# A two-layer graph attention kernel: weights loaded during the tables, the first layer's weights prepared on GpSimd, first gathers released by their indices alone

## The chip, the cores and the metric

One core of a Trainium2 chip runs the kernel. The metric is device time in microseconds from start to end of one execution. The core's engines run their own instruction streams and meet at semaphores: TensorE (PE, matrix products and transposes), VectorE (DVE), ScalarE (ACT), GpSimd (POOL) and SyncE (SP, which here only issues transfers). SP, ACT and GpSimd each issue DMA transfers, which run on the same 16 DMA engines.

## The reference

A graph has 12500 nodes with 256 features and 200000 edges, sorted by destination, each with one of 64 types. Two attention layers with 4 heads of 64 follow one another, each inside a residual sum and a layer norm.

```python
# layer 0, typed edges
enh = x + 0.1 * query_emb
Q, K, V = enh @ Wq + bq, enh @ Wk + bk, enh @ Wv + bv        # (N, 4, 64)
scores = einsum("ehd,ehd->eh", Q[dst], K[src] + 0.2 * rel_w[type]) / 8
w = segment_softmax(scores, dst)
msgs = segment_sum(w * V[src], dst)
x0 = layernorm(msgs @ Wo + bo + x) * gamma + beta
x = layernorm(x + x0)
# layer 1, plain edges and a loop on each node
xp = x @ W
alpha = leaky_relu((xp * att_src).sum(-1)[src] + (xp * att_dst).sum(-1)[dst], 0.2)
out = elu(segment_sum(segment_softmax(alpha, dst) * xp[src], dst) + bias)
x = layernorm(x + out)
```

## The kernel before

The kernel runs four stages one after another. Each is a `Stage`, which allocates its SBUF and PSUM tensors and semaphores; at its end all engines meet at a barrier and its semaphores are cleared. Tensors of the object `k` (`Kernel`) live through all four.

1. `make_tables` reads the edge lists as 105 rows of 1920 edges and makes the tables on which the later gathers work: `k.idx` (source indices by tile, turned by TensorE and copied by VectorE, L496), `k.first_row` and `k.match` (to HBM). A chain of checks ends in `k.flag` (L511). SP issues all loads (L429 to L435), ScalarE makes one cast (L460), GpSimd has no work.
2. `project_nodes` (98 blocks of 128 nodes) computes keys, values and queries. SP first issues eight weight loads (L547 to L553), then waits for VectorE's fill of `zero` (L631) and goes into its loop of x loads (L560), stores and clears of the sums. VectorE waits for all eight weights, spreads the query vector (L635); TensorE multiplies it by the weights (L608, L612) to fold it into the biases, and after VectorE's last scaling of the biases TensorE's loop begins with the transposes at L587. GpSimd adds beta to each x block (L672), into `k.x1`.
3. `attend_typed` is the first layer, over 521 tiles of 384 edges. GpSimd gathers three times 128 rows of `k.kv` per tile (L765) into one of eight row buffers; the ninth tile's gather waits until TensorE has aggregated the first. SP fetches index slices (L777), queries (L785), edge types and match rows (L801, L804). The order of each engine's work is written out by `interleave`: parts with a lag in tiles, and parts per node block every four or eight tiles that finish the block (norms, products with `Wo` and `W`).
4. `attend_plain` is the second layer, with the same gather scheme over `k.xp` (L1286).

What the change touches is how stage 3 starts. ScalarE issues its twelve weight loads as the stage opens (L1192 to L1201). VectorE fills buffers (L1080 to L1085), waits for all twelve, and prepares: the relation weights split in bfloat16 parts `rel_a`, `rel_b` (L1087 to L1100), the two biases in three bfloat16 rows each (L1103 to L1113, with fused multiply-adds), four products of `W` with the attention vectors (L1116) and two reductions of them into extra columns of `w1` (L1120). Each step waits for the one before it. Then VectorE raises `setup`, for which all the other engines wait ahead of their first step, GpSimd ahead of the first gather and SP ahead of the first query fetch:

```python
pool.wait_ge(setup, 1)
interleave(pool, FIRST, TilePart(0, gather))
```

## Time and profile before

| | us |
|---|---|
| median of three runs | 4633.29 |
| the three runs | 4626.58, 4633.29, 4635.58 |
| the profiled execution | 4628.61 |
| its span, first to last instruction | 4627.2 |

The stages as the timeline of that execution shows them:

| stage | opens at | first work of its main loop |
|---|---|---|
| tables | 1.02 | 8.30 (VectorE's chain) |
| projections | 30.03 | 44.75 (TensorE) |
| typed layer | 330.18 | 350.64 (first gather) |

A row of the timeline gives start, duration, engine, line of the kernel, operation, output and inputs with their sizes, how many instructions were merged (x4), and in brackets how long the engine had been idle and what released it. SPq, ACTq and the like are an engine's queue of DMA issues; their time is that of the issue, not of the transfer. A row of windows gives for each engine its busy time and instructions, in the order PE, PE's weight loads, VectorE, ScalarE, GpSimd, then the granted TensorE clock as a share of full speed, the DMA engines' busy share and the rate in GB/s. A row of a DMA queue gives packets, MB and the share of the 16 engines' time over the stretch. A row of waits gives who waited for whom, total time, times and longest.

### The profile page before, as it was taken

Reading aid. Unit: us, or ns where it says so; the run is one execution under the profiler, and the core shown is the slowest. Engines: PE = TensorE matmul, PEld = TensorE weight load, DVE = VectorE, ACT = ScalarE, POOL = GpSimd, SP = SyncE. Lnnn points to the kernel's source line nnn. Section 1 sums busy time; section 2 is a strip of 40 time slices with the busy share of each in tenths; the row PEclk is TensorE's granted clock in tenths of the full one; section 3 lists DMA queues with packets and bytes.
Section 4 is the critical chain, followed back from the end, with each engine's and each line's share of the span. In section 5 each row is a group of like instructions: output and inputs, shape, how many; then the busy total and the mean of one; then the engine's idle time right before and its main releaser. Section 6 shows DMA issues by size and latency. Waiting matters only on the chain. (4 is left out here: it accounts for less than half of the span.)

```text
span 4627.2 us, 149696 instructions
## 1 busy us (share of the span) xinstructions
PE 3929.3 (85%) x42462; PEld 2568.6 (56%) x42462; DVE 3415.2 (74%) x11602; ACT 2795.2 (60%) x7985; POOL 3143.2 (68%) x3229
## 2 busy tenths in 40 slices
PE   6988999999999999999996778778877877777874
PEld 4655555555555555555554556555555555555553
DVE  3235788777777778777775578888778778787777
ACT  2324555555555555555553677777777777777775
POOL 1217777777777777777772777777777777777773
PEclk9998999999999999999997677777778777787777
DMA  6878888888888888888884777777777777777774
GB/s 207 282 236 246 259 259 259 257 259 259 259 255 260 258 260 258 257 258 261 259 256 120 187 206 206 207 204 205 207 207 205 205 204 205 205 208 209 203 206 131
DMA packets 820558, 1052.06 MB, mean 227 GB/s; under 512 B 458633, under 2 KB 632338, under 8 KB 820464
## 3 DMA queue, kind: packets, MB, share of 16 engines
q0 software_dynamic: 225072, 726.83, 53.9%
q1 hardware_dynamic: 594078, 323.35, 27.0%
q10 hardware_dynamic: 1314, 0.99, 0.1%
q14 instruction: 80, 0.66, 0.0%
q8 instruction: 14, 0.23, 0.0%
HBM read 915.79 MB, written 133.39 MB: 227 GB/s over the span
## 5 line engine op out<-in xcount | busy, mean ns | idle before, releaser
L1286 POOL DMA_INDIRECT plain_rows<-xp,plain_index x1563 | 1559.8, 998 | 554.9 <-issue 440.8
L765 POOL DMA_INDIRECT typed_rows<-kv,typed_index x1563 | 1511.2, 967 | 626.2 <-issue 414.3
L1391 PE MATMUL plain_p_o<-plain_rows,plain_weight_t 128*64 128x130 f32 (+1 forms) x8336 | 856.5, 348 | 44.0 <-DVE plain_weight_t L1417 43.3
L1158 ACT ACTIVATE typed_weight<-typed_weight,typed_col 128x416 f32<-128x416 f32 x521 | 334.6, 642 | 855.0 <-DVE typed_col L991 809.5
L1378 PE MATMUL plain_p_s<-all_cst,plain_rows 128*128 128x128 f32 (+1 forms) x2084 | 455.0, 318 | 368.2 <-DMA plain_rows<-xp,plain_index 365.9
L1391 PEld LDWEIGHTS plain_p_o<-plain_rows,plain_weight_t 128*64 128x64 f32 (+1 forms) x8336 | 570.2, 169 | 203.8 <-issue 128.5
L1378 PEld LDWEIGHTS plain_p_s<-all_cst,plain_rows 128*128 128x128 f32 (+1 forms) x2084 | 335.2, 174 | 522.6 <-issue 504.8
L989 DVE CUSTOM_DVE_ANT_0 typed_weight<-typed_p_s,typed_far 128x416 f32<-128x416 f32 x521 | 305.1, 586 | 371.5 <-PE typed_p_s L874 347.8
L874 PE MATMUL typed_p_s<-typed_kt,typed_q 64*32 64x416 f32 x4168 | 472.4, 521 | 103.4 <-issue 73.0
L1424 DVE CUSTOM_DVE_ANT_0 plain_alpha<-plain_alpha,plain_far 128x416 f32<-128x416 f32 x521 | 310.0, 595 | 311.4 <-ACT plain_alpha L1540 296.4
L962 DVE TENSOR_TENSOR typed_kt<-typed_p_kt,typed_rel 128x768 f32<-128x768 f32 x521 | 494.7, 950 | 3.7 <-PE typed_p_kt L851 3.4
L1548 ACT ACTIVATE plain_weight<-plain_alpha,plain_col 128x416 f32<-128x416 f32 x521 | 331.4, 636 | 256.2 <-DVE plain_col L1433 250.4
L851 PE MATMUL typed_p_kt<-all_cst,typed_rows 128*128 128x128 f32 x3126 | 458.4, 283 | 6.8 <-DMA typed_rows<-kv,typed_index 6.3
L1559 ACT COPY plain_result<-plain_p_o 32x65 f32<-32x65 f32 x2084 | 425.4, 204 | 18.2
L889 PE MATMUL typed_p_o<-typed_rows,typed_weight_t 128*32 128x65 f32 (+1 forms) x16672 | 413.4, 225 | 3.0 <-ACT typed_result L1165 0.4
L1363 PE MATMUL plain_p_w<-all_cst,plain_weight 128*128 128x128 f32 x1563 | 360.5, 351 | 50.0 <-ACT plain_weight L1548 48.9
L851 PEld LDWEIGHTS typed_p_kt<-all_cst,typed_rows 128*128 128x128 f32 x3126 | 334.6, 142 | 98.2 <-issue 90.6
L1540 ACT ACTIVATE plain_alpha<-plain_p_s,plain_a_dst 128x416 f32<-128x416 f32 x521 | 316.7, 608 | 119.9 <-PE plain_p_s L1378 95.7
L1417 DVE COPY plain_weight_t<-plain_p_w 128x512 f32<-128x512 f32 x521 | 355.3, 682 | 32.1 <-PE plain_p_w L1364 20.5
L889 PEld LDWEIGHTS typed_p_o<-typed_rows,typed_weight_t 128*32 128x32 f32 (+1 forms) x16672 | 279.6, 108 | 168.2 <-issue 91.1
L1531 ACT ACTIVATE plain_far<-plain_match,all_cst 128x416 bf16<-128x416 uint8 x521 | 328.6, 631 | 9.0 <-DMA plain_match<-match 9.0
L1138 ACT ACTIVATE typed_far<-typed_match,all_cst 128x416 bf16<-128x416 uint8 x521 | 334.0, 641 | 0.0
(190 smaller groups left out, 6303.5 us busy)
## 6 DMA issues: line engine op xcount, KB each, us to landing
typed_match<-match SPq DMA_DIRECT2D x131, 208.0 KB
plain_match<-match SPq DMA_DIRECT2D x131, 208.0 KB
agg<-qkv_zero SPq DMA_DIRECT2D x98, 264.0 KB
typed_agg<-agg SPq DMA_DIRECT2D x98, 264.0 KB
plain_agg<-agg SPq DMA_DIRECT2D x98, 264.0 KB
kv<-qkv_kv SPq DMA_DIRECT2D x98, 258.0 KB
typed_kinds<-match SPq DMA_DIRECT2D x131, 192.0 KB
typed_rows<-kv,typed_index POOLq DMA_INDIRECT x1563
```

The lines of the kernel that those rows point to most:

```text
L765: pool.indirect_dma_start(rows[:, r, j, :], None, k.kv, bass.IndirectOffsetOnAxis(ap=index[:, g, at:at + 1], axis=0)).then_inc(rows_in[r], 16)
L851: last = pe.transpose(p_kt[:, pair, j * P:j * P + P], rows[:, t.slot(R), j, pair * P:pair * P + P], ident)
L874: last = pe.matmul(p_s[at:at + TN, 0:SLOTS], q[own, m, :, h // 2], kt[own, h // 2, lo:lo + SLOTS], start=True, stop=True, tile_position=(H ...
L889: last = pe.matmul(p_o[at:at + TN, 0:V], weight_t[0:e, t.slot(2), j * P + at:j * P + at + TN], v[:, D + V * h:D + V * h + V], start=j == 0 ...
L962: v.tensor_tensor(kt[:, :, lo:lo + MAIN], p_kt[:, :, 0:MAIN], both_pairs(0, MAIN), ALU.add).then_inc(kt_ready, 1)
L1158: act.activation(weight[:, c], weight[:, c], ACT.Exp, bias=col[:, t.slot(4), LOW:LOW + 1]).then_inc(exp_done, 1)
L1286: pool.indirect_dma_start(rows[:, r, j, :], None, k.xp, bass.IndirectOffsetOnAxis(ap=index[:, g, at:at + 1], axis=0)).then_inc(rows_in[r], 16)
L1363: pe.transpose(p_w[:, t.slot(2), j * P:j * P + P], weight[:, t.slot(2), j * P:j * P + P], ident)
L1378: last = pe.transpose(p_s[:, c, j * P:j * P + e], a_src[:, A_SRC:A_DST], ident[0:e, 0:e])
L1391: last = pe.matmul(p_o[at:at + HC, t.slot(2), 0:2 * V], weight_t[0:e, t.slot(2), j * P + at:j * P + at + HC], val[:, 2 * V * g:2 * V * g + ...
L1417: v.tensor_copy(weight_t[:, t.slot(2)], p_w[:, t.slot(2)]).then_inc(weight_t_ready, 1)
L1559: last = act.copy(result[at:at + TN, m, 0:V], p_o[at:at + TN, t.slot(2), V * (h % 2):V * (h % 2) + V])
```

## The change

- The twelve weight loads of the typed layer and the eight of the projections are issued by ScalarE in the tables stage, ahead of its cast. SP issues none of them any more.
- The tensors that they fill and the prepared weights move to `k`, or, for the projections, to a new object `Weights` that is freed ahead of the typed layer. The typed layer's scratch tensors (`att`, `prod`, `spare`, `rel_w`) become tensors of the tables stage.
- The preparation of the relation weights and biases and the four products run on GpSimd in the tables stage, each step of the first two after the completion of the last. The fused multiply-adds become a multiplication and an addition. The two reductions stay on VectorE, in the tables stage, ahead of its last two steps, behind a wait for the four products.
- In the typed layer VectorE keeps its fills but for three. GpSimd and SP no longer wait for `setup`; the first gathers wait for their index slice, the first fetches for nothing. TensorE and ScalarE still wait for `setup`.

```diff
 def gat_kernel(nc, inputs, out):
...
-            make_tables(k)
-            project_nodes(k)
+            with ExitStack() as front:
+                w = Weights(nc, front)
+                make_tables(k, w)
+                project_nodes(k, w)
...
@@ make_tables
+        @block.gpsimd
+        def _(pool):
+            count = 0
+
+            def init(instruction):
+                nonlocal count
+                instruction.then_inc(made, 1)
+                count += 1
+                pool.wait_ge(made, count)
+
+            for to in (k.bias_o, k.bias_1, k.ones):
+                init(pool.memset(to[:], 0.0))
+            init(pool.memset(k.ones[0:3], 1.0))
+            pool.wait_ge(weights_in, 16 * 12)
+            pool.wait_ge(consts_in, 16)
+            init(pool.tensor_scalar(rel_w[:, 0], rel_w[:, 0], 0.2, None, ALU.mult))
+            init(pool.tensor_copy(k.rel_a[:], rel_w[:, 0]))
+            init(pool.tensor_tensor(rel_w[:, 1], rel_w[:, 0], k.rel_a[:], ALU.subtract))
+            init(pool.tensor_copy(k.rel_b[:], rel_w[:, 1]))
+            init(pool.tensor_tensor(rel_w[:, 2], rel_w[:, 1], k.rel_b[:], ALU.subtract))
+            init(pool.tensor_copy(k.rel_a[REL:P], k.rel_b[REL:P]))
+            init(pool.tensor_copy(k.rel_b[:], rel_w[:, 2]))
+            init(pool.tensor_tensor(spare[:, 0], spare[:, 0], spare[:, 1], ALU.subtract))
+            init(pool.tensor_scalar(spare[:, 2], spare[:, 2], -1.0, None, ALU.add))
+            for whole, to in ((spare[:, 0], k.bias_o), (spare[:, 2], k.bias_1)):
+                init(pool.tensor_copy(to[0:3, 0:D], whole))
+                init(pool.tensor_tensor(whole, whole, to[0:3, 0:D], ALU.subtract))
+                init(pool.tensor_scalar(part[:, 0], to[0:3, 0:D], cst[0:3, C_ID:C_ID + 1], None, ALU.mult))
+                init(pool.tensor_copy(to[0:3, 0:D], whole))
+                init(pool.tensor_tensor(whole, whole, to[0:3, 0:D], ALU.subtract))
+                init(pool.tensor_scalar(part[:, 1], to[0:3, 0:D], cst[0:3, C_ID + 1:C_ID + 2], None, ALU.mult))
+                init(pool.tensor_tensor(part[:, 0], part[:, 0], part[:, 1], ALU.add))
+                init(pool.tensor_scalar(part[:, 1], whole, cst[0:3, C_ID + 2:C_ID + 3], None, ALU.mult))
+                init(pool.tensor_tensor(to[0:3, 0:D], part[:, 0], part[:, 1], ALU.add))
+            for side in range(2):
+                for a in range(2):
+                    pool.tensor_tensor(prod[:, side, a], k.w1[:, a, 0:D], att[:, side], ALU.mult).then_inc(prod_ready, 1)
+
         @block.scalar
         def _(act):
+            act.dma_start(k.wo[:], k.i["L0_gnn_Wo"].rearrange("(a p) n -> p a n", p=P)).then_inc(weights_in, 16)
...
+            for name, to in (("Wq", w.wq[:]), ("Wk", w.wkv[:, :, 0:D]), ("Wv", w.wkv[:, :, D:2 * D])):
+                act.dma_start(to, k.i["L0_gnn_" + name].rearrange("(a p) n -> p a n", p=P)).then_inc(k.project_in, 16)
...
             act.wait_ge(src_in, 16)
             act.copy(src_f[R], src[R]).then_inc(src_ready, 1)
...
             v.sem_inc(bad_ready, 1)
+            v.wait_ge(prod_ready, 4)
+            for side in range(2):
+                at = D + side * HEADS
+                then(v.tensor_reduce(k.w1[:, :, at:at + HEADS], prod[:, side].rearrange("p a (h c) -> p a h c", h=HEADS), AX, ALU.add))
             v.wait_ge(bad_in_row, 1)
...
@@ project_nodes
         @block.sync
         def _(sp):
-            for w, to in (("Wq", wq[:]), ("Wk", wkv[:, :, 0:D]), ("Wv", wkv[:, :, D:2 * D])):
-                sp.dma_start(to, k.i["L0_gnn_" + w].rearrange("(a p) n -> p a n", p=P)).then_inc(weights_in, 16)
...
@@ attend_typed, gpsimd
-            pool.wait_ge(setup, 1)
             interleave(pool, FIRST, TilePart(0, gather))
@@ attend_typed, sync
-            sp.wait_ge(setup, 1)
             interleave(sp, FIRST, TilePart(8, put_out), TilePart(0, fetch), BlockPart(0, 0, load), BlockPart(6, 10, store))
@@ attend_typed, vector
-            for to in (p_w, result, bias_o, bias_1, ones, message, message_t, x1, x1_t):
+            for to in (p_w, result, message, message_t, x1, x1_t):
                 init(v.memset(to[:], 0.0))
             init(v.memset(var[:], 1.0))
-            v.wait_ge(init_done, count)
-            init(v.memset(ones[0:3], 1.0))
-            v.wait_ge(weights_in, 16 * WEIGHTS)
...
             v.wait_ge(init_done, count)
             v.sem_inc(message_ready, TURN)
             v.sem_inc(summed, OUT + 1)
             v.sem_inc(x1_ready, TURN1)
             v.sem_inc(setup, 1)
@@ attend_typed, scalar
-            act.dma_start(wo[:], k.i["L0_gnn_Wo"].rearrange("(a p) n -> p a n", p=P)).then_inc(weights_in, 16)
...
```

## Rows read from the trace of the kernel before

**Rows 1.** The page: busy time of each engine over the span.
```profile
PE 3929.3 (85%) x42462; PEld 2568.6 (56%) x42462; DVE 3415.2 (74%) x11602; ACT 2795.2 (60%) x7985; POOL 3143.2 (68%) x3229
```

**Rows 2.** Windows by stage (busy us and instructions per engine, clock, DMA share, GB/s).
```profile
330.00:345.00 15.00, 0.00 (x0) 0.00 (x0) 8.46 (x31) 0.00 (x0) 0.00 (x0) 0.50 0.41 95
...
400.00:2440.00 2040.00, 1938.15 (x27515) 1164.71 (x27514) 1589.45 (x4468) 1113.06 (x2777) 1463.14 (x1514) 1.00 0.89 259
```

**Rows 3.** Timeline of the tables stage: start, us, engine, line, operation.
```profile
8.30 0.21 DVE L474 TENSOR_SCALAR tab_first<-tab_ends,all_cst 105x1 f32<-105x1 int32 x1 [7.02 <-DMA all_cst<-in_consts]
...
11.75 1.79 ACT L460 CAST tab_src_f<-tab_src 105x1920 f32<-105x1920 int32 x1 [9.45 <-DMA tab_src<-in_edges]
...
18.57 3.38 DVE L496 CAST all_idx<-tab_turned 128x420 int32<-128x420 f32 x4
...
23.38 2.16 DVE L504 TENSOR_TENSOR tab_gap<-tab_dst_f 105x1920 f32<-105x1920 f32 x1
...
28.90 0.14 DVE L511 TENSOR_SCALAR flag<-tab_worst 1x1 int32<-1x1 f32 x1
```

**Rows 4.** DMA while the tables load: one window, and SP's queue over 0 to 20.
```profile
5.00:6.00 1.00, 0.00 (x0) 0.00 (x0) 0.00 (x0) 0.00 (x0) 0.00 (x0) 1.00 1.20 255
...
q1 hardware_dynamic: 956, 2.78, 53.9%
```

**Rows 5.** Timeline of the start of the projections.
```profile
30.03 0.42 SPq L547 DMA_DIRECT2D qkv_wq<-in_L_gnn_Wq  x1
...
32.37 0.50 DVE L631 MEMSET qkv_zero<- 128x528 f32 x1
...
33.44 0.47 SPq L553 DMA_DIRECT2D qkv_bq<-in_L_gnn_bq  x1
33.96 0.47 SPq L560 DMA_DIRECT2D qkv_x<-in_x  x1
...
38.38 0.23 DVE L635 TENSOR_SCALAR qkv_query_all<-qkv_query 128x128 f32<-128x128 f32 x1 [5.51 <-DMA qkv_bq<-in_L_gnn_bq]
...
44.75 0.66 PE L587 MATMUL qkv_p_t<-all_cst,qkv_x 128*128 128x128 f32 x4 [1.16 <-DVE qkv_bq L642]
45.22 0.34 SPq L560 DMA_DIRECT2D qkv_x<-in_x  x1
...
47.31 0.73 POOL L672 TENSOR_TENSOR all_x<-qkv_x,qkv_beta 128x256 f32<-128x256 f32 x1 [4.46 <-DMA qkv_x<-in_x]
```

**Rows 6.** Timeline of the start of the typed layer.
```profile
330.18 1.89 SPq L777 DMA_DIRECT2D typed_index<-all_idx  x3
...
333.94 2.46 ACTq L1201 DMA_DIRECT2D typed_weight<-in_L_gnn_rel_w  x4
338.85 0.23 DVE L1087 TENSOR_SCALAR typed_weight<-typed_weight 128x128 f32<-128x128 f32 x1 [5.50 <-DMA typed_weight<-in_L_gnn_rel_w]
...
341.61 0.41 DVE L1105 TENSOR_TENSOR typed_kt<-typed_kt,typed_bias_o 3x256 f32<-3x256 f32 x1
...
346.58 1.41 DVE L1116 TENSOR_TENSOR typed_kt<-typed_w,typed_kt 128x256 f32<-128x256 f32 x4
348.02 1.28 DVE L1120 TENSOR_REDUCE typed_w<-typed_kt 128x8 f32<-128x512 f32 x2
...
350.64 1.09 POOL L765 DMA_INDIRECT typed_rows<-kv,typed_index  x1 [33.62 <-DVEq L1125]
...
352.04 0.95 POOL L765 DMA_INDIRECT typed_rows<-kv,typed_index  x1 [0.30 <-issue]
```

**Rows 7.** DMA of the typed start, 325 to 360: ACT's queue.
```profile
q10 hardware_dynamic: 1314, 0.99, 12.0%
```

**Rows 8.** Waits of GpSimd, 400 to 500 and 2000 to 2440: total, times, longest.
```profile
POOL typed_rows L765 <- issue: 23.6, 76, 0.6
...
POOL typed_rows L765 <- PE typed_p_o L889: 40.9, 46, 1.9
```

**Rows 9.** Groups of GpSimd's instructions before 330 us.
```profile
L672 POOL TENSOR_TENSOR all_x<-qkv_x,qkv_beta 128x256 f32 (+1 forms) x98 | 72.0, 735 | 244.3 <-DMA qkv_x<-in_x 244.3
```

More of the change, by code:

```diff
@@ new lines, in _ @@
+            act.dma_start(k.gamma[:], row(k, "L0_gnn_gamma")).then_inc(weights_in, 16)
+            for lo in range(0, P, REL):
+                for half in range(2):
+                    act.dma_start(rel_w[lo:lo + REL, 0, half * HC:half * HC + HC], k.i["L0_gnn_rel_w"]).then_inc(weights_in, 16)
+            for name, to in (("Wq", w.wq[:]), ("Wk", w.wkv[:, :, 0:D]), ("Wv", w.wkv[:, :, D:2 * D])):
+                act.dma_start(to, k.i["L0_gnn_" + name].rearrange("(a p) n -> p a n", p=P)).then_inc(k.project_in, 16)
@@ new lines, in _ @@
+            act.dma_start(w.bkv[:, 0:D], row(k, "L0_gnn_bk")).then_inc(k.project_in, 16)
+            act.dma_start(w.bkv[:, D:2 * D], row(k, "L0_gnn_bv")).then_inc(k.project_in, 16)
+            act.dma_start(w.beta[:], row(k, "L0_gnn_beta")).then_inc(k.project_in, 16)
+            with nc.allow_non_contiguous_dma(reason="two vectors, once"):
+                act.dma_start(w.query[:], k.i["L0_gnn_query_emb"].rearrange("(a p) -> p a", p=P)).then_inc(k.project_in, 16)
+                act.dma_start(w.bq[:], k.i["L0_gnn_bq"].rearrange("(a p) -> p a", p=P)).then_inc(k.project_in, 16)
@@ L545, in _ @@
         def _(sp):
-            for w, to in (("Wq", wq[:]), ("Wk", wkv[:, :, 0:D]), ("Wv", wkv[:, :, D:2 * D])):
-                sp.dma_start(to, k.i["L0_gnn_" + w].rearrange("(a p) n -> p a n", p=P)).then_inc(weights_in, 16)
-            sp.dma_start(bkv[:, 0:D], row(k, "L0_gnn_bk")).then_inc(weights_in, 16)
-            sp.dma_start(bkv[:, D:2 * D], row(k, "L0_gnn_bv")).then_inc(weights_in, 16)
-            sp.dma_start(beta[:], row(k, "L0_gnn_beta")).then_inc(weights_in, 16)
-            with nc.allow_non_contiguous_dma(reason="two vectors, once"):
-                sp.dma_start(query[:], k.i["L0_gnn_query_emb"].rearrange("(a p) -> p a", p=P)).then_inc(weights_in, 16)
-                sp.dma_start(bq[:], k.i["L0_gnn_bq"].rearrange("(a p) -> p a", p=P)).then_inc(weights_in, 16)
             def load(t):
@@ L1114, in _ @@
-            for side in range(2):
-                for a in range(2):
-                    init(v.tensor_tensor(prod[:, side, a], w1[:, a, 0:D], att[:, side], ALU.mult))
-            v.wait_ge(init_done, count)
-            for side in range(2):
-                at = D + side * HEADS
-                init(v.tensor_reduce(w1[:, :, at:at + HEADS], prod[:, side].rearrange("p a (h c) -> p a h c", h=HEADS), AX, ALU.add))
             v.wait_ge(init_done, count)
```

97 lines of the change are left out of this document (36 added, 61 removed).

## The prediction

> **What bounds the kernel now.** I read the page first, then windows by stage, then the timelines of the three starts that the change touches, and last the waits of GpSimd. The page gives no single bound: TensorE is busy 85%, VectorE 74%, GpSimd 68% [rows 1]. The windows show why that average says little here. In the first layer's steady part TensorE works 95% of the time and the DMA engines 89%, but from 330 to 345 us TensorE, ScalarE and GpSimd have nothing at all to do and VectorE alone works, 8.46 of 15 us [rows 2]. So the edit is worth what these starts are worth, and the reader is to look at three of them.
>
> The tables run VectorE as one chain from 8.30 (its inputs have landed) to 29.04, with ScalarE's cast and TensorE's turning of the sources ready when VectorE comes for them at 18.57 [rows 3]. The DMA engines are full meanwhile, share 1.20 in the window at 5 us [rows 4]. The projections open at 30.03 with weight loads; VectorE has its two fills done at 32.87 and then waits for the last weight until 38.38; TensorE's loop begins at 44.75 [rows 5]. The typed layer opens at 330.18; VectorE waits for its weights until 338.85, prepares them until 349.30, and only then the common signal lets GpSimd make the first gather, at 350.64 [rows 6].
>
> Who sets the pace after that first gather? A gather each 1.25 us (0.95 and a gap of 0.30, [rows 6]) makes 80 in 100 us, and from 400 to 500 there are 76 with nothing but issue in front of them [rows 8]: GpSimd's own rate fills the time. Later it is held by TensorE's release of buffers, 40.9 us out of 440 [rows 8]. A gather that starts earlier therefore moves the whole first layer, not only its first tile.
>
> **The change, part by part.**
>
> *Typed start, the gain.* Gathers now wait for their index slice alone. SP's three index fetches take 1.89 us from 330.18, the first being out by 330.8 [rows 6]. A small quiet load took 1.75 us from the end of its issue (45.56) to GpSimd's start (47.31) [rows 5], so the index is there at 332.6. GpSimd took 1.34 us from the end of VectorE's last reduction (349.30) to its first gather [rows 6]; I charge the same: first gather 333.9 where it was 350.64, a gain of 16.7. Bounds: no start delay gives 332.5 (18.1); a landing as slow as the projections' last vectors, 4.5 us (33.91 to 38.38, [rows 5]), gives 336.6 (14.0). VectorE's remaining fills end before 333.5, and then it needs only the relation kinds, 0.6 us of issue behind the indices; that lies beside the gathers of tile 0. SP's first query fetches leave earlier too and meet these gathers on the DMA engines. The cover is eight row buffers, 24 gathers or 30 us, before GpSimd needs anything back from TensorE. That also covers a microsecond or two of a later first tile, and TensorE's clock, granted at 0.50 (its 1.2 GHz level) before and presumably after.
>
> *Projection start, the gain.* SP's eight weight issues go, but its x loads still wait for VectorE's second fill, 2.84 us into the stage. VectorE goes on at 2.9 where it waited until 38.38 (8.35 in). From there to the loop 6.37 us (38.38 to 44.75) stay [rows 5]: bias products, additions, signals. Loop at 9.3 instead of 14.7: 5.4 gained. The x load leaves at 2.9 and even a loaded landing of 4.5 us is in before 9.3, with 1.4 to spare. The loop's pace is not touched.
>
> *Tables, the cost.* ScalarE's queue gets 20 issues. The twelve of the typed start ended at 336.40, 6.2 us after the stage opened [rows 6]; SP's eight took 3.9 [rows 5]; so ScalarE is free at about 11.5, just before its cast of the sources could start anyway (11.75, [rows 3]). VectorE's need of the turned sources is later still, at 18.57, hence nothing for that unless they slip by two microseconds more than VectorE does.
>
> The transfers are not free. SP's queue moved 956 packets in 53.9% of 16 engines over 20 us: 172 engine-us, 0.18 each [rows 4]. The first twelve weights were 1314 packets in 12.0% of 35 us: 67 engine-us, 0.051 each [rows 7]. The other eight have 1664 rows by their shapes, at the same price 85. The tables' inputs and the twelve weights need (172+67)/16 = 15 us from about 2 us on: the weights are in at 17 plus about 1 at the latest, and at 2+8.4+1 = 11.4 if they get half of each engine. Their packets are short, so they get less than half while SP's last; I take 16. VectorE's inputs slip by between 0 and 4.2 (67/16); I take 2. All twenty are in by about 23, before the projections.
>
> Then GpSimd's chain of 31 instructions, the first 27 each after the completion of the one before. GpSimd's one elementwise row here is 0.735 us for 128x256 with two inputs [rows 9]; VectorE's two-input 256-column step was 0.41 [rows 6]: 1.8 times. VectorE's chain for the same work ran from 338.85 to 348.02 [rows 6], 9.2 us; at 1.8 that is 16.5, and two fused steps in each of two biases become two plain ones, 4 x 0.73 = 2.9 more. I take 19: from 16 to 35. Bounds: VectorE's pace, 9.2+4x0.3 = 10.4; or the step of an indirect DMA, 1.25 (from 0.95 and 0.30), 38.8. GpSimd, not VectorE (29.04+2), is then what ends the tables. Behind the new wait on its products VectorE has queued two reductions (1.28 us, [rows 6]) and the two flag steps, together 1.8 with gaps. The tables end at 36.8 against 29.04: 7.8 lost. Lower bound 1.3 (the chain hidden, only the reductions added), upper bound 18+38.8+1.8-29.04 = 29.6.
>
> The Trainium skill speaks against this placing. Its page "GPSIMD Engine Reference", section "Key points", says that GpSimd shares SBUF interfaces with VectorE and is held up by VectorE's instructions with two SBUF inputs or in a two-port mode. VectorE has such a step, L504, 2.16 us, within GpSimd's chain [rows 3]; an estimate by that page: 2.2 more lost, 10.0 instead of 7.8. No row of before sets the two side by side.
>
> *Sum.* 7.8 - 5.4 - 16.7 = -14.3. The profiled execution took 4628.61 (span 4627.2, 1.4 around it), so 4614.3 in its terms; it lies 4.7 below the median of 4633.29, in whose terms it is 4619.0.
>
> **Rivals.**
>
> *The tables hide it all.* The weights land at 12 and GpSimd runs near VectorE's pace, done before VectorE. Then only 1.3 to 4 are lost: 1.3-5.4-16.7 = -20.8, 4612.5. For it: VectorE's chain is 21 us long. Against: DMA is full, and a two-input step costs 1.8 times as much.
>
> *A slow GpSimd chain.* Steps of 0.8 to 1.25 us through waiting on itself: 13 to 28 lost, -9 to +6, around 4630. For it: its start delay of 1.34 and gaps of 0.30. Against: 0.735 is a whole step with two inputs, and most of the 31 have one input or half the columns.
>
> *The other side: slower.* The same chain, in the tables' last stretch, with nothing beside it. It outweighs both gains when it costs over 22.1, that is when a step exceeds (22.1+29.04-1.8-16)/31 = 1.08 us; past 0.2% slower (31.4 lost) when it exceeds 1.38. At 1.5: 16+46.5+1.8-29.04 = 35.3 lost, +13.2, 4646.5. No row has a GpSimd step that long.
>
> *The head start is given back.* If TensorE or the DMA engines set the first layer's pace from its first tile, they could absorb 16.7: 7.8-5.4 = +2.4, 4635.7. For it: TensorE at 95%. Against: the waits of GpSimd [rows 8], and TensorE has nothing to do before the rows arrive, so it too starts earlier.
>
> **How the numbers follow.** About 0.2% (9.3 us) is what a measurement of this kernel can tell from no change. Forecast (tables cost 4 to 13) 0.62; hidden 0.12; slow chain with 13 to 31 lost 0.15; slower 0.03; given back 0.07; 0.01 for what I do not see. Faster: the first two, 0.74. Slower: 0.04. Same: 0.22. The range goes from the hidden case with the gathers' upper bound and a little scatter, 4609, to the middle of the slow chain, 4631; it leaves out the far ends of the last three, under 0.2.
>
> **What the changed profile would show.** GpSimd's products end at 31 to 40 us and VectorE's two reductions directly after them, waiting on GpSimd; VectorE's first step at 8.3 to 12.5; the first projection transposes 9.3 us after the stage opens, not 14.7; the first typed gather about 3.7 us after its stage opens, not 20.5, and gathers 1.25 us apart behind it. The prediction is wrong if GpSimd's steps are not near 0.6 on average, if the twelve weights land far from 16, or if gathers stall on TensorE within the first 100 us.

## The result, and the profile after

The changed kernel takes 4679.51 us (median of 4 executions, 4674.36 to 4686.34); the kernel before took 4629.93 (4 executions, 4624.70 to 4635.58). The ratio is 1.0108, with a 95% interval of 1.0088 to 1.0127: 49.6 us slower, where 4619.0 in a range of 4609 to 4631 was forecast. The profiled execution took 4677.25 us over a span of 4675.9.

The page after, against [rows 1]; below it the queue of instructions (packets, MB, share), which had 80 packets and 0.66 MB before:

```profile
PE 3940.7 (84%) x42462; PEld 2574.9 (55%) x42462; DVE 3404.3 (73%) x11571; ACT 2786.7 (60%) x7985; POOL 3155.4 (67%) x3264
...
q14 instruction: 215, 1.76, 0.1%
```

No engine's busy time grew by more than 12.1 us, so most of the 49 us are waiting. Windows by stage, against [rows 2]:

```profile
330.00:345.00 15.00, 4.25 (x16) 2.03 (x14) 3.76 (x12) 1.23 (x4) 2.41 (x3) 0.79 0.34 101
400.00:2440.00 2040.00, 1935.60 (x27444) 1162.59 (x27440) 1591.10 (x4464) 1111.89 (x2775) 1459.69 (x1511) 1.00 0.89 258
```

The first layer's steady part is as it was. The tables, against [rows 3] (timeline, of all engines):

```profile
9.02 3.23 ACTq L539 DMA_DIRECT2D front_wkv<-in_L_gnn_Wv  x1
10.26 0.21 DVE L561 TENSOR_SCALAR tab_first<-tab_ends,all_cst 105x1 f32<-105x1 int32 x1 [9.01 <-DMA all_cst<-in_consts]
...
17.01 1.28 ACT L547 ACT_TABLE_LOAD   x1 [17.01 <-issue]
...
18.31 1.79 ACT L547 CAST tab_src_f<-tab_src 105x1920 f32<-105x1920 int32 x1
...
19.29 0.83 POOL L503 TENSOR_SCALAR tab_rel_w<-tab_rel_w 128x128 f32<-128x128 f32 x1 [17.09 <-DMA tab_rel_w<-in_L_gnn_rel_w]
...
28.90 2.45 POOL L519 TENSOR_TENSOR tab_part<-tab_part 3x256 f32<-3x256 f32 x1
...
37.65 0.71 POOL L519 TENSOR_TENSOR tab_part<-tab_part 3x256 f32<-3x256 f32 x1
...
40.25 2.76 POOL L524 TENSOR_TENSOR tab_prod<-all_w,tab_att 128x256 f32<-128x256 f32 x4
...
43.05 1.41 DVE L599 TENSOR_REDUCE all_w<-tab_prod 128x8 f32<-128x512 f32 x2 [9.68 <-POOL tab_prod L524]
...
44.78 0.14 DVE L602 TENSOR_SCALAR flag<-tab_worst 1x1 int32<-1x1 f32 x1
```

VectorE waits 9.68 us for GpSimd's products, and the tables end at 44.92 instead of 29.04. ScalarE's table load (L547), which ran at 1.02 before, now stands behind its 20 DMA issues and takes 1.28 us ahead of the cast. The starts of the projections' loop and of the typed layer, against [rows 5, 6]:

```profile
54.42 0.66 PE L663 MATMUL qkv_p_t<-all_cst,qkv_x 128*128 128x128 f32 x4 [1.16 <-DVE front_bq L718]
...
339.20 1.89 SPq L839 DMA_DIRECT2D typed_index<-all_idx  x3
...
341.99 1.16 POOL L828 DMA_INDIRECT typed_rows<-kv,typed_index  x1 [15.57 <-DMA typed_index<-all_idx]
```

The first gather is 8.65 us earlier than before (350.64, [rows 6]); TensorE's first transposes of gathered rows are 7.9 earlier (359.11 to 351.24). So up to there the change gained. Now the second layer, which the change doesn't touch; its first gather, before and then after:

```profile
2533.20 0.95 POOL L1286 DMA_INDIRECT plain_rows<-xp,plain_index  x1 [78.75 <-DMA plain_index<-all_idx]
```
```profile
2529.32 0.94 POOL L1300 DMA_INDIRECT plain_rows<-xp,plain_index  x1 [80.26 <-DMA plain_index<-all_idx]
```

From there to the end of the span it takes 4627.2 - 2533.2 = 2094.0 us before and 4675.9 - 2529.3 = 2146.6 after: 52.6 us lost, more than the whole result. VectorE's waits for nothing that the profile shows ("issue"), 3000 to 4000 us (total, times, longest), before:

```profile
DVE plain_weight_t L1417 <- issue: 5.3, 12, 0.4
```

After, with the queue of instructions in the same window, in which the kernel before has none:

```profile
DVE plain_weight_t L1431 <- issue: 78.6, 16, 6.4
DVE plain_kept L1497 <- issue: 27.4, 16, 2.6
```
```profile
q14 instruction: 78, 0.64, 0.2%
```

VectorE stops 16 times in 1000 us, once in every pass of its loop over 16 tiles, and some 40 KB of instructions are fetched in each pass (0.64 MB over 16). One such stop, in VectorE's timeline:

```profile
3073.68 0.17 DVE L1482 TENSOR_TENSOR plain_share<-plain_scaled,plain_total 128x8 f32<-128x8 f32 x1
3080.25 0.69 DVE L1431 COPY plain_weight_t<-plain_p_w 128x512 f32<-128x512 f32 x1 [6.40 <-issue]
...
3082.12 0.15 DVE L1448 SCALAR_TENSOR_TENSOR plain_col<-plain_col 128x1 f32<-128x1 f32 x1
3084.20 0.42 DVE L1497 SCALAR_TENSOR_TENSOR plain_kept<-plain_h,all_x 128x256 f32<-128x256 f32 x1 [1.93 <-issue]
```

L1431 is the loop's first operation: the 6.40 us, one of the longest of these stops, are the jump back. Then a few instructions run for 2.0 us, and VectorE stops again.

**Where the loop stands.** In VectorE's compiled program (64 bytes an instruction) the body of this loop is 337 instructions long. Before, it stood at 2819 to 3155. The change took out 29 instructions net ahead of it (waits and signals counted), so it stands at 2790 to 3126. Counted in blocks of 256 from the program's start, the first is in two blocks (11 and 12), the second in three (10 to 12), with only 26 instructions in the first of them. The trace doesn't show these positions; they are counted in the program. The Trainium skill, page "Runtime: NRT & Kernel Launch", section "Instruction fetch mechanics", says that the instruction memory of most engines (TensorE's is larger) is two lines of 256 instructions, and that a taken branch to a line that isn't there waits for its fetch. By that rule a loop in two blocks stays in place and one in three is fetched in each pass; the trace, with 78 packets against none, agrees. Three blocks would be 48 KB a pass, and the trace has 40; which part isn't fetched anew I don't know.

### The profile page after: what moved, and what is told of

It reads as the page before. It is cut to its first block and busy times, and to the rows that moved or that the text cites. A ratio compares the mean times of both kernels' runs of the same rounds, so it can differ in the third digit from the quotient of the medians.

```text
span 4675.9 us, 149715 instructions
## 1 busy us (share of the span) xinstructions
PE 3940.7 (84%) x42462; PEld 2574.9 (55%) x42462; DVE 3404.3 (73%) x11571; ACT 2786.7 (60%) x7985; POOL 3155.4 (67%) x3264
## 5 line engine op out<-in xcount | busy, mean ns | idle before, releaser
L1405 PE MATMUL plain_p_o<-plain_rows,plain_weight_t 128*64 128x130 f32 (+1 forms) x8336 | 870.1, 352 | 265.2 <-DVE plain_weight_t L1431 264.3
L1392 PE MATMUL plain_p_s<-all_cst,plain_rows 128*128 128x128 f32 (+1 forms) x2084 | 440.4, 317 | 115.3 <-DMA plain_rows<-xp,plain_index 114.7
L1431 DVE COPY plain_weight_t<-plain_p_w 128x512 f32<-128x512 f32 x521 | 355.7, 683 | 141.8 <-issue 132.0
L1377 PEld LDWEIGHTS plain_p_w<-all_cst,plain_weight 128*128 128x128 f32 x1563 | 201.9, 169 | 259.7 <-ACT plain_weight L1562 164.7
```

Source lines behind the costliest of these rows:

```text
L1377: pe.transpose(p_w[:, t.slot(2), j * P:j * P + P], weight[:, t.slot(2), j * P:j * P + P], ident)
L1392: last = pe.transpose(p_s[:, c, j * P:j * P + e], a_src[:, A_SRC:A_DST], ident[0:e, 0:e])
L1405: last = pe.matmul(p_o[at:at + HC, t.slot(2), 0:2 * V], weight_t[0:e, t.slot(2), j * P + at:j * P + at + HC], val[:, 2 * V * g:2 * V * g + ...
```

## The experiments

Eighteen runs were made, of eight kernels. Seven runs were on chips on which the kernel before takes 4627.86, 4630.76 or 4633.85 us; they are told first, one execution each. Eleven were on chips on which it takes 6110 to 6243 us; they are told at the end of this section. The four executions of the kernel before in the result lie 11 us apart, so between two single executions a difference of the whole time below some 11 us says nothing. The second layer's own time, read from the trace (its first gather to the end of the span), scatters less: in the five kernels with its loop in two blocks it is 2092.0 to 2097.7 us.

### The changed kernel, its loop at the old place

```diff
@@ attend_plain, vector, behind v.sem_inc(setup, 1)
+            for _ in range(29):
+                v.memset(unused[:, _:_ + 1], 0.0)
```

> The changed kernel, VectorE's second loop at its old place (2819 to 3155). On a chip where the kernel before takes 4630 us: theory, place in the program, 4624 to 4627 us with a second layer of 2094 us (the run without the bias split took 4616.1, and the split costs 9.6). Rival, leaving out the split is what helped there: 4660 us or more.

4629.12 us beside 4627.86, the second layer 4627.7 - 2530.0 = 2097.7 us. VectorE's waits in 3000 to 4000 (and no instruction packets there):

```profile
DVE plain_weight_t L1432 <- issue: 5.7, 13, 0.4
```

29 added instructions that do nothing of use take 48 us off the changed kernel, in which the start of the stages, the moved buffers and the transfers are as they were: none of these is the cause. That the memsets help by moving the loop, and not by standing there, the next two experiments show.

### The same move without the change

```diff
@@ project_nodes, vector, behind the fill of zero
+            for _ in range(90):          (120 in before_pad227)
+                v.memset(unused[:, _:_ + 1], 0.0)
@@ attend_plain, vector, behind v.sem_inc(setup, 1)
+            for _ in range(107):
+                v.memset(unused[:, _:_ + 1], 0.0)
```

The kernel before with 197 memsets (three blocks, 56 of the loop's instructions in the first):

> The kernel before with its second loop on VectorE at 3016 to 3352 (three blocks of 256). On a chip where the kernel before takes 4630 us: theory, place in blocks, about 4680 us, second layer about 2146 us; rival, the cost is in something that the change did, 4630 to 4640 us and 2094 us.

4654.78 us beside 4633.85; the second layer 4653.3 - 2535.3 = 2118.0. The loss came, but 24 us of it and not the 52 that I expected. VectorE's waits in 3000 to 4000, then its jump back in the timeline, show the difference:

```profile
DVE plain_weight_t L1421 <- issue: 80.9, 16, 6.2
```
```profile
3079.40 0.17 DVE L1472 TENSOR_TENSOR plain_share<-plain_scaled,plain_total 128x8 f32<-128x8 f32 x1
3083.81 0.69 DVE L1421 COPY plain_weight_t<-plain_p_w 128x512 f32<-128x512 f32 x1 [4.24 <-issue]
...
3085.75 0.42 DVE L1487 SCALAR_TENSOR_TENSOR plain_kept<-plain_h,all_x 128x256 f32<-128x256 f32 x1
```

No second stop, and the first is no shorter (5.1 us on average, 4.9 in the changed kernel): with 56 instructions ahead of the next block VectorE seems to be busy until it is there. So I moved the loop by 30 more, to 3046 to 3382, with 26 in the first block as in the changed kernel:

> The kernel before with 120 memsets in the projections and 107 in the second layer's preparation: the loop at 3046 to 3382, three blocks of 256, with 26 instructions in the first, as in the changed kernel (2790 to 3126). With 56 there (before_pad197_look) VectorE lost 5.1 us at the head of each pass, and the second layer took 2118.0 us; the second wait of the changed kernel, 1.7 us at L1497 behind those 26 instructions, did not come. Theory, the whole loss is the two waits: both come back, 80 and 27 us in 3000:4000, the second layer takes 2140 to 2150 us and the whole 4677 to 4685. Rival, half of the loss in the second layer is of something else that the change did: the second wait may come, but the second layer stays at about 2118 us and the whole near 4656.

4695.44 us beside 4627.86, the second layer 4694.1 - 2534.3 = 2159.8, 10 us above the range that I had written down. Both stops are back, the second ahead of the same operation (`plain_kept`) as in the changed kernel:

```profile
DVE plain_weight_t L1421 <- issue: 78.3, 15, 6.3
DVE plain_kept L1487 <- issue: 31.9, 15, 2.7
DVE plain_moments L1499 <- issue: 3.8, 15, 0.3
```

The kernel before, none of whose work is changed, loses 68 us by the place of a loop. Its first layer is as long as before (first transposes at 359.10, the second layer's first gather at 2534.3), so neither the memsets nor the first layer's loop have a part in it. Why it loses 13 us more in the second layer than the changed kernel with the same 26 instructions stays open.

### The changed kernel with twelve memsets

The edit is that of the first experiment with 12 instead of 29: the loop at 2802 to 3138, 14 instructions in its first block.

> The changed kernel with 12 memsets: three blocks still, but with 14 instructions of the loop in the first. In the changed kernel's trace VectorE ran its 26 in 2.0 us and then waited 1.93, so the next block came 3.95 us after the first. Theory: 14 instructions are run in about 1.2 us, the second wait is about 2.7 us a pass instead of 1.7, the first about 4.9 as before, and the second layer takes 2146 us or up to 30 us more (32 passes by 1 us). Rival, any memset ahead of the loop helps: 2094. Rival, the second wait costs nothing: 2146 or below.

4727.29 us beside 4627.86, the second layer 4725.3 - 2528.85 = 2196.5. It is dearer still, 50 us above the changed kernel and 20 above the top of what I expected, so memsets as such cure nothing. The second stop that I expected did not come: the first grew instead.

```profile
3081.48 0.17 DVE L1483 TENSOR_TENSOR plain_share<-plain_scaled,plain_total 128x8 f32<-128x8 f32 x1
3089.95 0.69 DVE L1432 COPY plain_weight_t<-plain_p_w 128x512 f32<-128x512 f32 x1 [8.30 <-issue]
...
3091.89 0.42 DVE L1498 SCALAR_TENSOR_TENSOR plain_kept<-plain_h,all_x 128x256 f32<-128x256 f32 x1
```
```profile
DVE plain_weight_t L1432 <- issue: 128.8, 15, 10.0
```

The second wait may then be part of the first, VectorE setting out only when the next block too is there; no run tests that.

The six together (waits of VectorE on "issue" at the lines shown above, in 3000 to 4000, over the passes in that window):

| kernel | loop at | blocks | in the first | waits a pass | second layer |
|---|---|---|---|---|---|
| before | 2819 | 2 | 253 | 0.3 | 2094.0 |
| changed, 29 memsets | 2819 | 2 | 253 | 0.4 | 2097.7 |
| before, 197 memsets | 3016 | 3 | 56 | 5.1 | 2118.0 |
| changed | 2790 | 3 | 26 | 6.6 | 2146.6 |
| before, 227 memsets | 3046 | 3 | 26 | 7.6 | 2159.8 |
| changed, 12 memsets | 2802 | 3 | 14 | 8.6 | 2196.5 |

The layer has 521 tiles, some 32 passes. At 5.1 us a pass VectorE stands still for 162 us and the layer grows by 24: VectorE has gaps of its own (busy 799 of 1000 us before, 3000 to 4000), and I take it that the tiles in flight bridge most of the stop. At 8.6 it stands for 275 and the layer grows by 102. Of what comes on top of 5.1 us a pass half to seven tenths are paid: 2159.8 - 2118.0 = 41.8 for 32 x 2.5 = 80, and 2196.5 - 2118.0 = 78.5 for 32 x 3.5 = 112. The other three kernels with the loop in two blocks, told below, have second layers of 2092.0 (release alone), 2095.3 (no bias splits) and 2097.5 us (loads early).

### What the tables' end waits for

The kernel of the first experiment without the two bias splits, so that both bias rows stay zero:

```diff
@@ make_tables, gpsimd
-            for whole, to in ((spare[:, 0], k.bias_o), (spare[:, 2], k.bias_1)):
-                init(pool.tensor_copy(to[0:3, 0:D], whole))
...
-                init(pool.tensor_tensor(to[0:3, 0:D], part[:, 0], part[:, 1], ALU.add))
```

> The changed kernel with the 29 memsets (loop at its old place), and GpSimd's splitting of the two bias rows in three parts (18 instructions, L513 to L521 twice, 24.43 to 40.17 us in the profile after) left out, so both bias rows stay zero. Theory, GpSimd's chain ends the tables: its four products start at about 24.4 instead of 40.25 and end at 27.2, VectorE's reductions then follow its own work at about 33.4 instead of 43.05, and the flag is written at about 35.3 instead of 44.9: 9.6 us earlier, and everything after it. Of the 15.9 us that the tables grew the other 6.2 us stay: they come from VectorE's and ScalarE's own delay behind the twenty loads. Rival, the loads' landing or VectorE's delay alone set it: the flag stays at 44 to 45 us. Rival, GpSimd's work slowed VectorE by a shared port: VectorE's L591 and L592 (2.16 and 2.15 us) get shorter and the flag ends before 35.

```profile
29.36 2.15 DVE L582 TENSOR_REDUCE tab_count<-tab_gap 105x1 f32<-105x1920 f32 x1
...
32.07 1.41 DVE L589 TENSOR_REDUCE all_w<-tab_prod 128x8 f32<-128x512 f32 x2 [0.15 <-DVE tab_bad L584]
...
33.80 0.14 DVE L592 TENSOR_SCALAR flag<-tab_worst 1x1 int32<-1x1 f32 x1
```

The flag is written at 33.94, 11.0 us earlier than in the changed kernel, and the whole took 4616.13 us beside 4630.76. GpSimd's chain set the end of the tables. Of the 11.0 us some 9.6 are its share, as expected; the rest is that VectorE's own steps came 1.45 us earlier in this execution (L582 at 29.36, the same step at 30.81 in the changed kernel). The 15.9 us that the tables grew are then VectorE's 9.7 us of waiting for the products, 1.4 for the two reductions and 5.2 of delay ahead of them (L592 at 30.81, L505 at 25.57 before), less 0.5 that VectorE had waited for TensorE at that place before. VectorE's long steps were not shorter without GpSimd beside them (2.16 and 2.15 both times), but GpSimd's L519 took 2.45 us where it ran beside VectorE's L591, which has two inputs, and 0.71 where it did not: 1.7 us for that collision (L591 ends at 30.77, L519 at 31.35). The prediction gave 2.2 for it by the Trainium skill's page "GPSIMD Engine Reference", section "Key points", and did not take it into the sum; the trace agrees with the rule.

### The release alone

```diff
@@ attend_typed of the kernel before, gpsimd and sync
-            pool.wait_ge(setup, 1)
...
-            sp.wait_ge(setup, 1)
```

> The kernel before without GpSimd's and SyncE's wait for VectorE's preparation. In release_only the weights landed 12.1 us after the stage opened (342.80) instead of 8.5, behind the gathers' rows, and the first match on TensorE came at 354.7 instead of 350.3. Theory: that is so here too, the first tile starts 3 to 4 us later than in the kernel before, but eight tiles of rows lie ready, so 6 to 13 us of the 17 us of the gathers' lead are left: 4617 to 4625 us. Rival, the late preparation eats it all: 4630 to 4634 us.

4628.13 us beside 4627.86: nothing of the 6 to 13 us that I expected. The first gather came 15.6 us earlier, and the weights that VectorE needs came later (338.85 before, [rows 6]):

```profile
335.01 1.09 POOL L765 DMA_INDIRECT typed_rows<-kv,typed_index  x1 [16.58 <-DMA typed_index<-all_idx]
...
344.32 0.23 DVE L1085 TENSOR_SCALAR typed_weight<-typed_weight 128x128 f32<-128x128 f32 x1 [10.13 <-DMA typed_weight<-in_L_gnn_rel_w]
...
358.41 1.54 PE L849 MATMUL typed_p_kt<-all_cst,typed_rows 128*128 128x128 f32 x6
...
378.01 0.94 POOL L765 DMA_INDIRECT typed_rows<-kv,typed_index  x1 [12.33 <-PE typed_p_o L887]
```

In the kernel before the same transposes had waited for their rows:

```profile
359.11 1.54 PE L851 MATMUL typed_p_kt<-all_cst,typed_rows 128*128 128x128 f32 x6 [6.27 <-DMA typed_rows<-kv,typed_index]
```

The stage opened 0.8 us later than in [rows 6], so the weights landed 4.6 us later within it, beside the gathers' rows and the query fetches. VectorE's preparation ended 5.6 us later (354.85, 349.30 before). That took up nearly all of the 6.27 us for which TensorE no longer had to wait: its first transposes are 0.7 us earlier. GpSimd filled its eight buffers and then stood for 12.33 us ahead of its 25th gather, until TensorE had released the first; that gather is at 378.01, where it was at 380.84 before. So its lead of 15.6 us was down to 2.8, and the second layer's first gather is at 2534.76 (2533.20).

What counts is when the first tile starts on TensorE, not when the first gather leaves. The first layer's length shows it: from the first transposes to the second layer's first gather it is 2174.1 us in the kernel before, 2178.1 in the changed one, and 2175.2 to 2179.0 in the seven runs on these chips, whether the first gather leads these transposes by 8.5 us or by 23.4 us.

### The loads early, the preparation where it was

ScalarE issues the twenty loads in the tables, but behind its cast and with the projections' eight first. VectorE prepares the weights in the typed layer as in the kernel before; the waits of GpSimd and SP for it are gone. The tensors that the loads fill share their place with `kt` and `weight`, which are now allocated from the tables on. VectorE's instructions are as many as before, so its loops stand where they stood.

```diff
@@ make_tables, scalar
             act.wait_ge(src_in, 16)
             act.copy(src_f[R], src[R]).then_inc(src_ready, 1)
+            for name, to in (("Wq", w.wq[:]), ("Wk", w.wkv[:, :, 0:D]), ("Wv", w.wkv[:, :, D:2 * D])):
+                act.dma_start(to, k.i["L0_gnn_" + name].rearrange("(a p) n -> p a n", p=P)).then_inc(k.project_in, 16)
...
+            act.dma_start(m.wo[:], k.i["L0_gnn_Wo"].rearrange("(a p) n -> p a n", p=P)).then_inc(k.typed_in, 16)
...
```

> The twenty loads behind ScalarE's cast, VectorE's preparation in the typed stage, no waits for it, loops in two blocks. On a chip where the kernel before takes 4630 us: theory, the 12 us that the first match leads by on TensorE stay to the end, or grow to 16, 4614 to 4618 us; rival, the lead is lost on the way, about 4625 us.

```profile
11.87 1.79 ACT L494 CAST tab_src_f<-tab_src 105x1920 f32<-105x1920 int32 x1 [9.56 <-DMA tab_src<-in_edges]
...
29.48 0.14 DVE L563 TENSOR_SCALAR flag<-tab_worst 1x1 int32<-1x1 f32 x1
...
39.79 0.66 PE L624 MATMUL qkv_p_t<-all_cst,qkv_x 128*128 128x128 f32 x4 [1.17 <-DVE front_bq L679]
...
324.43 1.89 SPq L806 DMA_DIRECT2D typed_index<-all_idx  x3
327.18 1.10 POOL L795 DMA_INDIRECT typed_rows<-kv,typed_index  x1 [15.13 <-DMA typed_index<-all_idx]
...
336.86 1.28 DVE L1148 TENSOR_REDUCE mid_w<-mid_kt 128x8 f32<-128x512 f32 x2
```

4615.86 us beside 4633.85, 18.0 less, as the theory had it. The cast starts at 11.87 as before, the tables end 0.6 us later than before instead of 15.9, the projections' loop starts 5.0 earlier, and VectorE has the weights prepared 13.7 us after the stage opens instead of 19.1. TensorE's first transposes are at 341.70, 17.4 earlier, and of this lead 16.3 are there at the second layer's first gather (2516.94). It is the fastest version of this section that keeps the whole computation.

### The same kernels on chips where the kernel before takes over 6100 us

> The changed kernel with 29 memsets of one element (to a buffer that nothing reads) at the end of VectorE's preparation of the second layer, so that its loop there stands in the program where it stood before (instructions 2819 to 3155 instead of 2790 to 3126). Theory, place in the program: VectorE's loop is fetched anew in each pass because of where it stands; with the old place the second layer takes 2094 us again instead of 2146.6, VectorE's waits 'issue' of 78.6 and 27.4 us in 3000:4000 fall to under 10 us, the instruction queue is empty there, and the whole lands near 4625 us (4677 less 52.6). Rival, rhythm: the earlier start or the moved buffers put the second layer in another rhythm; nothing changes here, about 4677 us. Rival, clock or transfers: also about 4677 us.

> The changed kernel with only 12 such memsets: the loop stands at 2802 to 3138. Divided into blocks of 256 instructions counted from the program's start that is still three blocks (10 to 12), as in the changed kernel, where 2819 to 3155 is two. Theory, place in blocks: still about 4677 us and a second layer of about 2146 us. Rival, any memset ahead of the loop (a delay, a settled order) cures it: about 4625 us. Rival, the cost falls evenly with the shift: 12 of 29, about 4655 us.

> The kernel before with 90 such memsets in the projections (where VectorE waits for the weights) and 107 in the second layer's preparation: the loop of the second layer goes from 2819 to 3155 (two blocks of 256) to 3016 to 3352 (three, 11 to 13); the first layer's stays in two. Nothing of the change is in it. Theory, place in blocks: a second layer of about 2146 us instead of 2094, in all about 4683 us, with the waits 'issue' of about 78 and 27 us in 3000:4000 and instruction packets in the queue. Rivals that lay the cost to something in the change (buffers, early start, weights in memory): no more than the memsets themselves, under 10 us, so 4630 to 4640 us.

> The kernel before with 90 memsets in the projections and 40 in the second layer's preparation: the loop stands at 2949 to 3285, two blocks (11 and 12). Control for the memsets themselves. Theory, place in blocks: 4630 to 4637 us, a second layer of about 2094 us, no instruction packets in 3000:4000. Rival, the further the loop stands from its place of before the dearer: about two thirds of the loss of the kernel with 197, so 4665 us if that stands at 4683.

> The kernel before with two lines taken out: GpSimd's and SyncE's wait for VectorE's preparation in the first layer. Weights are loaded where they were and VectorE prepares them as before (its preparation ends at 349.3 us in the profile before, the first transposes start at 359.1). Theory, first tiles wait for the gathers: the first gather leaves about 2.8 us after the stage opens (at about 333 instead of 350.6), but VectorE can't take a tile before 349.3, so the first transposes start at about 350 instead of 359.1, and the run is 9 to 10 us shorter: about 4620 us. Rival, the gathers alone set the pace and eight tiles of buffers take up the lead: 16 to 17 us shorter, about 4613. Rival, VectorE catches up anyway: no change, 4630. The second layer stays at about 2094 us (loop at 2819 as before).

> All twenty weight loads go out on ScalarE during the tables, but behind its cast, the projections' eight first; VectorE prepares the first layer's weights where it did before, in the typed stage; GpSimd's and SyncE's waits for it are gone. VectorE's loops keep their places in the program. Theory (the three parts of the change that paid, without the two that cost): tables end at about 29 us as before instead of 44.9, the first matmul of the projections' loop about 5 to 6 us earlier than before (about 39), the first gather about 3 us after the typed stage opens and VectorE's preparation ends there about 7 us after it opens instead of 19, so in all 20 to 23 us below the kernel before: about 4608 us. Rival, the typed layer's lead is lost on the way: only the 5 to 6 us of the projections and half the lead, about 4618. Rival, twenty loads beside the tables' own still delay them: tables end at 33 or later, about 4613 to 4622 us.

In the kernel before with 130 memsets 90 stand in the projections and 40 in the second layer; the other edits are shown above.

Four of them ran again, one a third time, on chips of the same kind:

> The same kernel as after_pad29 (VectorE's loop at 2819 to 3155 by 29 memsets), measured where the kernel before takes 4630 us. The run without the bias split, at 4616 us, already stands 14.6 us below the kernel before with this placement; with the split back 9.6 us are given back. Theory, place in the program: 4625 to 4627 us, the second layer 2094 us. Rival, rhythm: 4677 us.

> The same kernel as after_pad12 (loop at 2802 to 3138, three blocks of 256), measured where the kernel before takes 4630 us. Theory, place in blocks: about 4677 us, with 2 to 3 instruction packets per pass of the loop as in the changed kernel. Rival, any memset cures it: 4625. Rival, evenly with the shift: 4655.

> The same kernel as before_pad197 (the kernel before, loop at 3016 to 3352, three blocks), measured where the kernel before takes 4630 us. Theory, place in blocks: about 4680 us, with VectorE's waits 'issue' in each pass of the loop. Rival, the cost is in something that the change did (buffers, early start): 4630 to 4640 us.

> The same kernel as early_loads (twenty loads behind ScalarE's cast, VectorE prepares in the typed stage, waits gone, loops where they stood), measured where the kernel before takes 4630 us. Its stages up to the first transposes depend little on the rest: the projections' loop started at 39.1 (before 44.75) and the first match on TensorE at 338.3 (before 350.3). Theory: that lead of 12 us stays, or grows to 16 by the gathers' head start; 4614 to 4618 us. Rival, the lead is lost on the way: about 4625.

> The same kernel as before_pad197 (the kernel before, VectorE's second loop moved by memsets to 3016 to 3352, three blocks of 256). Where the kernel before takes 4630 us: theory, place in blocks, about 4680 us with a second layer of about 2146 us; rival, the cost is in something that the change did, 4630 to 4640 us. Where the kernel before takes over 6100 us again: both theories, a ratio of 1.000 to 1.003, and it tells nothing.

Measured, as ratios to the kernel before with their 95% intervals:

| kernel | first | again | packets of instructions |
|---|---|---|---|
| changed, 29 memsets | 0.9997 (0.9983 to 1.0011) | 0.9994 (0.9985 to 1.0003) | 80 |
| changed, 12 memsets | 0.9978 (0.9964 to 0.9992) | 0.9981 (0.9968 to 0.9994) | 215 |
| before, 197 memsets | 1.0020 (1.0002 to 1.0038) | 1.0022 (1.0007 to 1.0037), third 1.0019 (1.0003 to 1.0035) | 215 to 217 |
| before, 130 memsets (two blocks) | 1.0009 (0.9996 to 1.0022) | | 82 |
| release only | 0.9984 (0.9969 to 0.9999) | | 80 |
| early loads | 0.9963 (0.9948 to 0.9979) | 0.9960 (0.9949 to 0.9972) | 80 |

None of the times that I wrote down could come on these chips, where the kernel before takes 1500 to 1600 us more. What the runs show is that the fetches follow the place of the loop on every chip, 215 to 217 packets in three blocks and 80 to 82 in two, while the price is nearly gone: the kernel with 12 memsets, 100 us slower than the kernel before above, is 0.2% faster than it here, and 197 memsets cost 0.2%. The gain of the early loads is there on both kinds, 19.3 and 24.8 us here. The long times came from the chips numbered 1 and 3 and in the seven runs the short ones from 4, 13 and 15, one execution each; whether it is the chip isn't shown. The kernel itself runs otherwise. In the changed kernel with 29 memsets GpSimd issues 525 instructions in 1000 us of the first layer (737 in the same kernel on the other chips), and in the second VectorE stands on "issue" at another line, in two blocks as in three. Windows, then VectorE's waits in 4000 to 6000:

```profile
1000.00:2000.00 1000.00, 855.10 (x9562) 462.34 (x9562) 573.72 (x1578) 398.47 (x986) 504.44 (x525) 0.95 0.69 184
4000.00:6000.00 2000.00, 1394.16 (x8982) 992.93 (x8980) 1168.74 (x4706) 1087.54 (x3413) 1106.87 (x1124) 0.62 0.59 151
```
```profile
DVE plain_alpha L1439 <- issue: 304.8, 144, 8.2
DVE plain_weight_t L1432 <- issue: 6.6, 15, 0.4
```

With 12 memsets, the same waits on the same chip:

```profile
DVE plain_alpha L1439 <- issue: 209.6, 116, 6.2
DVE plain_weight_t L1432 <- issue: 126.1, 19, 7.7
```

The stop at the jump back is there (7.7 us at the longest), and the wait at the other line shrinks by 95 us where it adds 120: most of it lies in time that VectorE waits anyway. What holds these chips back I did not find out.

## Why the prediction was wrong

The step that failed is one that the prediction never took: it counted what each removed instruction costs, and not where the rest then stands. It says of the second layer nothing at all, so its sum holds 0 for a stage that lost 52.6 us: with VectorE's loop in three blocks of 256 instructions instead of two, VectorE stood 6.6 us a pass (3000 to 4000) waiting for instructions, in some 32 passes. With the 3.9 us that were gained up to the second layer this is the whole result of the profiled executions, 52.6 - 3.9 = 48.7 (4675.9 - 4627.2). No view of the kernel before shows such a loss coming, but two facts did lie open: the removed instructions (29 on VectorE ahead of the loop), and that the steady second layer, 3000 to 4000, had no instruction packets, so that it had something to lose.

- **Projections, 5.4 gained.** The loop started 9.7 us later than before while the tables ended 15.9 later: 6.2 gained. Right.
- **Typed start, 16.7 gained.** First gather 2.79 us after the stage opened where it was 20.46: 17.7. Right in size. The reason was not: that a gather which starts earlier moves the whole first layer fell with the release alone, which moved the gather by 15.6 us and the end by nothing. The prediction's own reading, that GpSimd's rate fills the time from 400 to 500 us, did not carry that far: it named gathers that stall on TensorE in the first 100 us as a sign of being wrong, and in the release alone one stalled for 12.33 us, while in the changed kernel none did. In the changed kernel VectorE's preparation was out of the stage too, and so TensorE's first rows came earlier by nearly as much, 16.9 us within the stage. So the term came out right for a reason that the prediction didn't give.
- **Tables, 7.8 lost.** 15.9. The 8.1 us more are two mis-sized terms. The twelve weights landed at 19.3 (forecast 16). GpSimd's chain took 23.7 us (19), 0.76 a step and not 0.6: its steps with one input and a scalar took 0.83 to 0.92, above the 0.735 that I took for the dearest kind, and L519 lost 1.7 beside VectorE. A third was wrong and cost nothing: ScalarE was not free at 11.5 but at 17.0, for single issues took 3.23 and 2.36 us while the transfers were busy, and the table load of 1.28 us came behind them. Its cast went from 11.75 to 18.31, and VectorE waited 2.75 us for the turned sources; but it had 9.68 us to wait for GpSimd afterwards. The loss is that of the rival of a slow GpSimd chain, 13 to 28, by steps a little below its 0.8 and a later start.
- **Sum.** With these, 15.9 - 6.2 - 17.7 = -8.0, which is the -8.65 of the first gather but for a projections' loop that was 0.65 us shorter. 7.9 us of it are there at TensorE's first transposes, 3.9 are left at the second layer's first gather. With the loop back at its old place the kernel takes 4629.12 beside 4627.86, and 0.9994 to 0.9997 of the kernel before elsewhere: no difference. There 4 to 5 us of the lead go in the first layer (2178.9 for 2174.1) and 3.7 in the second (2097.7 for 2094.0); kernels with the same loops scatter by as much, so no cause can be given for these.

The median of 4679.51 us lies 48.5 above the top of the range, 4631, and the chance of slower stood at 0.04, for a GpSimd chain with steps above 1.38 us. That mechanism did not come (0.76 a step): the slower result has another cause.

## What to carry to other kernels

When an edit adds or removes instructions ahead of a loop, look where the loop's body stands in the engine's program before and after: here a body of 337 instructions in three blocks of 256 cost 24 to 102 us against two, the more the fewer of its instructions were in the first. That was so where the kernel takes 4630 us; on the chips where it takes over 6100 the fetches were the same and cost 0.2% at most. A queue of instructions that moves packets in a steady loop, with "issue" waits at the loop's first line once a pass, is the sign, and a few instructions of padding ahead of the loop are a test and a cure. And an early transfer is worth its lead only if what it feeds can start: move the loads and the wait together. The loads did no harm behind ScalarE's last work of the tables; ahead of it, and with the preparation on GpSimd, they ended that stage 15.9 us later.

## What the runs showed of the hardware

- A jump back of VectorE to a block that had to be fetched stopped it for 4.9 to 5.2 us on average (6.4 at most) where 26 or 56 instructions stood in that block, and for 8.6 (10.0 at most) where 14 did. With 26 instructions there VectorE went on in the next block 3.95 us after it had begun in the first (3080.25 to 3084.20).
- ScalarE's last six DMA issues of weight loads took 0.45 to 3.23 us each in the changed kernel; the same six, issued behind its cast, took 0.45 to 0.49.
- On GpSimd a step with a scalar took 0.86 to 0.92 us for 3x256 and a step with two inputs 0.66 to 0.71, while casts took 0.39. On VectorE the same kinds took 0.27 to 0.34, 0.41 and 0.28 (timeline of the kernel before, 339 to 346).
- With gathers and query fetches released at the stage's start, weights loaded in the same stage landed 4.6 us later.
- GpSimd's work beside a two-input step of VectorE took longer: 2.45 us instead of 0.71 for L519, and a gather's issue took 1.54 and 1.45 us instead of 0.95 beside VectorE's four products of `W` (release alone at 352.82, loads early at 336.20).
